# Moving four stores of weight sums ahead of input and context loads on SyncE's DMA queue (cross-attention and a ternary feed-forward net, one core)

## The reference

```
x = x + attention(layernorm(x), ctx)     # gelu(q ctx^T) * (q ctx^T), then times ctx
x = x + ffn(layernorm(x))

ffn:  h = silu((x w1^T) * s1) * ((x w2^T) * s2)          # 256 -> 1024
      h = gelu((h h1^T) * a)                              # 1024 -> 1024
      h = gelu((h h2^T) * b)                              # 1024 -> 1024
      return (h w3^T) * s3                                # 1024 -> 256
```

## Time and profile before

| What | Value |
| --- | --- |
| Median of 3 runs | 330.27 us |
| Lowest and highest | 329.37 and 330.33 us |
| Span of the profiled execution, first to last instruction | 328.7 us |
| PE busy | 320.8 us, 98% of the span |
| DVE busy | 263.9 us, 80% |
| ACT busy | 218.2 us, 66% |
| DMA queue of POOL (q0) and of SP (q1) | 37.75 MB and 22.11 MB |
| HBM read, written | 49.36 MB, 6.29 MB |

### The profile page before, as it was taken

The page is one execution under the profiler, slowest core; times in us unless marked ns, Lnnn a source line. Parts: engine busy times, 40 slices in busy tenths (PEclk is TensorE's granted clock), DMA queues, the critical chain, the costliest instruction groups (busy, mean ns, idle before and its releaser), DMA issues.

```text
span 328.7 us, 4727 instructions
## 1 busy us (share of the span) xinstructions
PE 320.8 (98%) x1628; PEld 271.5 (83%) x1628; DVE 263.9 (80%) x494; ACT 218.2 (66%) x367; POOL 41.7 (13%) x67
## 2 busy tenths in 40 slices
PE   7899999999999999999999999999999999999994
PEld 5799888788878888889998888888887888888994
DVE  4877996886995999997679475498899798987594
ACT  3567556574895876869835545977589687875840
POOL 5355010100000013003020002000000000100000
PEclk9999999999999999999999999999999999999999
DMA  6699999977738654755007033335575853443003
GB/s 205 243 282 284 206 272 325 417 262 277 234 139 296 215 193 128 208 182 177 11 2 255 3 128 128 131 127 194 214 241 183 296 217 128 128 136 122 0 30 107
DMA packets 23213, 60.22 MB, mean 183 GB/s; under 512 B 1680, under 2 KB 7568, under 8 KB 20624
## 3 DMA queue, kind: packets, MB, share of 16 engines
q0 software_dynamic: 13440, 37.75, 37.7%
q1 hardware_dynamic: 9744, 22.11, 19.9%
HBM read 49.36 MB, written 6.29 MB: 169 GB/s over the span
## 4 chain that ended last, share of the span: by engine, by line
PE 86%; DMA 6%; DVE 5%; issue 1%; POOL 1%; ACT 0%; DVEq 0%; POOLq 0%
PE P L1308 58%; PE P L1260 14%; PE P L1337 9%; DMA blocks_h<-H 3%; PE P L1224 2%; DMA WR<-blocks_h 2%; PE P L1216 2%; PE P L1232 1%; DVE TR L910 1%; DMA xs<-in_x 1%; DVE st L794 0%; DVE H L1039 0%; DVE H L1037 0%; DVE H L1035 0%; DVE H L1034 0%
## 5 line engine op out<-in xcount | busy, mean ns | idle before, releaser
L1308 PE MATMUL P<-TR,WR 128*128 128x512 f32 x896 | 206.0, 391 | 0.3 <-DMA WR<-blocks_h 0.3
L1308 PEld LDWEIGHTS P<-TR,WR 128*128 128x128 f32 x896 | 167.5, 188 | 36.6 <-DVE H L926 1.1
L603 ACT ACTIVATE TR<-H 128x512 fp32r<-128x512 f32 x112 | 68.1, 626 | 30.0 <-DVE H L905 27.3
L910 DVE TENSOR_TENSOR TR<-H,TR 128x512 fp32r<-128x512 f32 x112 | 73.8, 687 | 8.5 <-ACT TR L603 6.8
L1260 PE MATMUL P<-X,W 128*128 128x512 f32 (+1 forms) x320 | 62.5, 351 | 0.0
L1260 PEld LDWEIGHTS P<-X,W 128*128 128x128 f32 x320 | 51.7, 189 | 7.6
L905 DVE TENSOR_TENSOR H<-H 128x512 f32<-128x512 f32 x64 | 42.0, 685 | 0.0
L883 DVE SCALAR_TENSOR_TENSOR H<-P,sc,SLY 128x512 f32<-128x512 f32 (+1 forms) x40 | 25.2, 638 | 18.6 <-PE P L1260 10.0
L593 ACT ACTIVATE SLY<-P,sc 128x512 f32<-128x512 f32 (+1 forms) x40 | 23.9, 603 | 17.9 <-PE P L1260 15.3
L617 ACT ACTIVATE H<-P 128x512 f32<-128x512 f32 x48 | 27.8, 593 | 10.8 <-PE P L1308 10.8
L637 ACT ACTIVATE H<-H,sc 128x512 f32<-128x512 f32 x40 | 27.4, 715 | 10.7 <-DVE H L926 10.7
(11 more groups left out here) (74 smaller groups left out, 183.6 us busy)
## 6 DMA issues: line engine op xcount, KB each, us to landing
WR<-blocks_h POOLq DMA_DIRECT2D x16, 1024.0 KB, 4.8
WR<-in_h POOLq DMA_DIRECT2D x12, 1024.0 KB, 5.2
H<-in_h POOLq DMA_DIRECT2D x8, 512.0 KB, 16.1
blocks_h<-H SPq DMA_DIRECT2D x4, 1024.0 KB, 9.9
SLY<-in_h SPq DMA_DIRECT2D x8, 512.0 KB, 4.2
SLY<-in_w SPq DMA_DIRECT2D x6, 512.0 KB, 4.0
W<-in_w POOLq DMA_DIRECT2D x2, 1024.0 KB, 8.8
WR<-in_w POOLq DMA_DIRECT2D x2, 1024.0 KB, 5.2
```

The lines of the kernel that those rows point to most:

```text
L603: eng.activation(TR[:, f % RING, 0, :], operand(c, L, s, kk), ACT.Copy).then_inc(s_hi, 1)
L910: eng.tensor_tensor(TR[:, f % RING, 1, :], operand(c, L, s, kk), TR[:, f % RING, 0, :].bitcast(f32), ALU.subtract).then_inc(s_lo, 1)
L1308: out_ = eng.matmul(bank(c, L, s, m)[:, :], WR[r % WRING][:, at:at + 128], TR[:, f % RING, h, :], start=(s in FRESH[L] and kk == 0 and h = ...
```

## The change

The four stores of weight sums change their places in SP's program. Stores 0, 1 and 2 now stand ahead of the inputs of batches 4 and 5 and the contexts of tile 2; store 3 stands ahead of the inputs of batches 6 and 7 and the contexts of tile 3. No other engine's program changes, and no transfer is added or removed.

```diff
             eng.wait_ge(s_w12[1], 16)
             load_cf(1)
             load_ct(1)
+            sums_out(0)
+            sums_out(1)
+            sums_out(2)
             load_x(4)
             load_x(5)
             load_cf(2)
             load_ct(2)
-            sums_out(0)
+            sums_out(3)
             load_x(6)
             load_x(7)
-            sums_out(1)
             load_cf(3)
             load_ct(3)
-            sums_out(2)
-            sums_out(3)
             eng.dma_start(s3b[:, :], s3.broadcast_to([128, D])).then_inc(s_s3, 16)
             for i in range(9):
                 load_check(i)
```

## The result

The changed kernel takes 334.49 us (median of 4 runs, 334.32 to 334.92) against 329.93 us for the kernel before in the same job (329.37 to 330.33). The ratio is 1.0136, with a 95% interval of 1.012 to 1.0152: slower by 4.6 us, between 4.0 and 5.0. Later jobs with up to 29 runs of the kernel before put its median at 329.9 to 330.1. The profiled execution has a span of 333.0 us against 328.7.

A forecast was written before the change was run, and what follows sets the result against it. PE was taken as the bound, busy 320.8 of 328.7 us, with DVE reaching product 6 just in time. The sum was 330.27 - 0 + 3.2 = 333.5 us, range 331.6 to 335.6 for 8 in 10.

The forecast's parts named there:

- The wait at 63.75: PE before product 1, waiting for POOL's block: goes, 0.3 us, at most 0.7, counted as nothing since product 6 waits for DVE.
- the 2 to 5 us of the sum: Store 1 on SP's queue: lands some 2 to 5 us earlier with the loads gone from ahead of it.
- The late inputs and contexts: x4 to x7 and contexts of tiles 2 and 3: 30 us or more of products cover them, cost nothing as loads.
- Check load 0 is late: Four loads behind store 3 delay check load 0; ACT, DVE and PE at product 6 pass 3.2 us on; chance 0.76.
- The slacks of 2.3 and 1.4 us: PE at product 3's fourth bank loses the delay less 2.3 us, at product 4 the delay less 1.4.
- The price of the delay, 3.2 us: Check load 0 behind 1.03 MB of four loads at 318 GB/s: 3.2 us later, with 2.5 and 4.0 as ends.
- The 2.4 us that I set beside this term: The four loads priced by the skill page's fit alone, bytes over 436 GB/s: 2.4 us, sum 332.7.
- The check load did not overtake: Rival, not slower: the short check load overtakes in SP's queue and lands in time, 330.1 us; chance 0.14.
- My figure of 2.0 us for the issues alone: SP's issues of two inputs and two contexts: by these alone check load 0 would be 2.0 us late.
- The faster rival: Transfers around 70 us thin out, check load 0 lands before 74.9, the kernel wins 1.4 us: 328.9; chance 0.04.
- The clock did not fall: Rival, much slower: pauses before products 3, 4 and 6 drop PE's clock to 1.2 GHz, 335.5 us; above 335, chance 0.06.
- The other reading of that rival: POOL's load slows the check load more than allowed, giving the same 335.5 us; above 335, chance 0.06 for both readings.

The follow-up runs named there:

- the first part alone: Against the kernel before, only stores 0 to 2 go ahead of x4, x5 and the contexts of tile 2; store 3 stays by `s3b`: 330.24 us, ratio 1.0007.
- the kernels at 329.6 and 329.7: The changed kernel or the first part alone, with check load 0 issued ahead of store 3 or the loads behind it, magnitude 0 one product later, or both: 329.61 to 329.69 us.
- magnitude 0 later: Against the changed kernel, the magnitude and test of check load 0 stand one product later in ACT's and DVE's programs, DMA order untouched: 329.68 us, ratio 0.9984.
- the small POOL load: Against the changed kernel, POOL's load of product 4's weights moves an eighth of its columns, so results are not the reference's: 332.84 us, ratio 1.0081.
- two loads: Against the changed kernel, cf3 and ct3 go ahead of store 3, so only x6 and x7 (512 KB) stand behind it: 331.69 us, ratio 1.0042.
- check load 0 ahead of the loads: Against the changed kernel, check load 0 is issued right behind store 3, ahead of x6, x7, cf3, ct3 and `s3b`: 329.61 us, ratio 0.9985.

## Why the prediction was right, and where its size was off

*The wait at 63.75 goes and gives nothing.* Right. Store 1 no longer holds POOL's load, which is issued 3.7 us earlier (53.84 against 57.50), within the 2 to 5 us of the sum though short of the landing near 52; PE starts product 1 without a wait, and the first part alone has a ratio of 1.0007.

```profile
53.84 1.65 POOL L471 DMA_DIRECT2D WR<-blocks_h  x3 [10.27 <-DMA blocks_h<-H]
```

With DVE out of the way too (the kernels at 329.6 and 329.7) the ratios are 0.9984 to 0.9997, a gain of 0.1 to 0.5 us, this wait included.

*The late inputs and contexts cost nothing as loads.* Right: with magnitude 0 later, all of them are issued as late as in the changed kernel and the time is 329.68.

*Check load 0 is late, and ACT, DVE and PE pass the delay on in full.* Right, and to the hundredth: magnitude 0, `lo`, the totals and product 6 all moved by 4.35 or 4.36 us in the changed kernel; 2.15 and 2.14 with the small POOL load; 1.33 and 1.32 with two loads. The slacks of 2.3 and 1.4 us before products 3 and 4 that I took from the rows also hold: the two kernels with delays of 1.33 and 2.15 have no break at product 3's fourth bank on PE, the one with 2.15 has one of 0.63 us at product 4, and with 4.36 there are both.

*The price of the delay, 3.2 us.* This term was mis-sized: it is 4.05 us by the clock of store 3 and 4.36 by position. I priced the four loads by their bytes at 318 GB/s and let POOL's load stand only as a reason for the upper end. Both halves of that were off. The 318 GB/s come from a stretch with the engines at 0.85 (and the 257 from one at 0.80), so there were gaps to fill; with the engines full, from 74 to 80 us, the changed kernel moved 398 to 422 GB/s. That made the price too high. And POOL's queue, counted as nothing in the sum, put 0.75 MB more in front of magnitude 0 (1.07 - 0.32), which made it too low: 2.2 us of the delay go when its load is made small. How the 4.05 us split between the four loads and POOL's bytes is not shown more exactly than that. So that 333.5 came near 334.49 is partly luck: two errors stood against each other, and the kernel before measured 329.93, 0.34 us under the 330.27 that I added to. The change itself was forecast at 3.2 us and measured at 4.6. The 2.4 us that I set beside this term rest on a fit that the Trainium skill (DMA: Bandwidth & Descriptors, Anatomy of one DMA) gives for transfers issued from GpSimd. These four are issued from SP, and no run shows the fit for them. A slip without effect: `s3b` before landed at 67.83 + 6.9 = 74.7, not near 74.9.

*The rivals.* The check load did not overtake: in the changed kernel it landed at 72.0 + 8.3 = 80.3, behind all six transfers of its queue from store 3 on. The four loads were there by 76.1 (the last, `ct`, 70.93 + 5.2), `s3b` at 79.1 (71.47 + 7.6). My figure of 2.0 us for the issues alone was low as well: check load 0 was issued 3.5 us later. The faster rival falls with the same landing, which would have had to come before 74.9. The clock did not fall: its granted level is 1.00, the upper one of 2.4 GHz, in every stretch of 2 us of the changed kernel from 68 to 100 us. The stretches in which the three pauses lie read

```profile
78.00:80.00 2.00, 1.63 (x8) 1.01 (x6) 0.00 (x0) 0.00 (x0) 0.76 (x1) 1.00 1.03 422
80.00:82.00 2.00, 0.07 (x1) 0.07 (x1) 0.00 (x0) 1.67 (x3) 0.00 (x0) 1.00 1.10 329
...
88.00:90.00 2.00, 1.36 (x6) 1.05 (x6) 2.00 (x4) 2.00 (x5) 0.75 (x1) 1.00 0.77 238
...
96.00:98.00 2.00, 1.27 (x6) 0.59 (x5) 2.00 (x5) 2.00 (x5) 0.54 (x1) 1.00 0.00 0
```

The other reading of that rival, POOL's load slowing the check load more than I allowed, has something in it: it did slow it, by 2.2 us, but the whole delay of 4.36 us stayed under the 5.3 of my range.

## What to carry to other kernels

A gap in the chain that ended last is worth only what the next engine lets through: before a wait is taken away, look for the next place where the engine meets another one with nothing left over, here product 6, some 30 us later. A queue that only issues DMAs has a critical item like any engine; find the transfer that an in-order engine waits for with work queued behind it, and keep everything that nobody waits for behind that one, not ahead. The cost of a transfer moved ahead of it is not its bytes alone but also what the delayed one then runs into on the other queue.

## What the runs showed of the hardware

The price of bytes ahead in a queue was not linear. 512 KB more ahead of check load 0 cost 0.94 us, 1008 KB cost 4.05 us, and with POOL's load cut to an eighth the 1008 KB cost 1.86 us. Counted by what all queues moved up to the start of magnitude 0, the three are closer: against the 2.47 MB of before, 0.32 MB more went with 0.94 us, 0.85 MB with 1.86 us and 1.84 MB with 4.05 us, which is 340, 457 and 454 GB/s. So the bytes to count were those of both queues, the later check loads included. These are quotients from one execution each. And the rate in one stretch differed much with the engines equally busy: in the changed kernel, with a DMA share near 1 in both,

```profile
70.00:72.00 2.00, 2.00 (x11) 1.65 (x10) 2.00 (x4) 2.00 (x4) 0.54 (x1) 1.00 0.99 236
72.00:74.00 2.00, 2.00 (x10) 1.69 (x9) 1.48 (x3) 2.00 (x5) 0.00 (x0) 1.00 1.01 364
```

236 and 364 GB/s (the last column; the one before it is the DMA share). The slow stretch lies some 3 us behind the issue of store 3 in other kernels too (237 GB/s with check load 0 ahead of the loads), but not in all (305 GB/s with the first part alone). Its cause was not tried.
